# Attention: half of the indexer's head weighting moved from VectorE to GpSimd

## The reference, cut to what matters

```
iq = (x @ w_iq.T + b_iq).reshape(B, S, 4, 64); ik = x @ w_ik.T + b_ik; iw = x @ w_iw.T + b_iw
head_scores  = relu(einsum('bqhd,bkd->bhqk', iq, ik))       # four heads, 256 x 256 each
index_scores = einsum('bhqk,bqh->bqk', head_scores, iw)     # weigh each head per row, add the four
top_idx = top_k(index_scores, 32)                           # the 32 largest of each row stay
logits = (Q @ K.T) * scale, -inf outside top_idx            # Q, K with rotary embedding
x = x + (softmax(logits) @ V) @ w_o.T + b_o
```

## Time and profile before

| | |
|---|---|
| median of 3 runs | 1355.04 us |
| the profiled execution | 1355.75 us |
| its span (first to last instruction) | 1353.9 us |
| PE / ACT / DVE / POOL busy over the span | 78% / 55% / 69% / 60% |
| attention in the trace | from about 16.6 to 210.4 us |
| DVE busy from 100 to 140 us, inside attention | 38.68 of 40 us |
| POOL busy in the same 40 us | 14.62 us |
| TensorE's granted clock from 30 to 180 us | 1.00 |

### The profile page before, as it was taken

How to read it: one execution, slowest core, us unless ns; L and a number is a source line. 1 busy time by engine, 2 the same in 40 slices (tenths; PEclk the granted TensorE clock), 3 DMA queues, 4 the chain that set the end, 5 groups by cost and what they waited for, 6 DMA issues and landing times. The chain is left out here.

```text
span 1353.9 us, 20321 instructions
## 1 busy us (share of the span) xinstructions
PE 1060.0 (78%) x4202; PEld 618.8 (46%) x4203; DVE 932.1 (69%) x2276; ACT 745.8 (55%) x1821; POOL 817.2 (60%) x602
## 2 busy tenths in 40 slices
PE   3898874349999955888989888897775319999995
PEld 3666653227777731333333333333223215555563
DVE  4999997503333333799999999989997625555573
ACT  3777754325555547858586776757531115555542
POOL 1443320667317557877886888788781567437276
PEclk9999985569999976989999999899897559999997
DMA  8994000136425425344435443443540026535335
GB/s 243 161 147 139 1 1 1 41 53 88 71 56 89 84 31 110 85 141 133 155 116 168 124 157 124 137 159 114 185 140 1 31 54 94 85 73 96 79 67 103
DMA packets 136875, 133.22 MB, mean 98 GB/s; under 512 B 14578, under 2 KB 117602, under 8 KB 136674
## 3 DMA queue, kind: packets, MB, share of 16 engines
q1 hardware_dynamic: 107106, 115.55, 32.3%
q0 software_dynamic: 29696, 16.86, 9.8%
HBM read 98.66 MB, written 31.60 MB: 96 GB/s over the span
## 5 line engine op out<-in xcount | busy, mean ns | idle before, releaser
L1569 POOL TENSOR_TENSOR ss_HC<-ss_Hs,ss_Cb 128x512 f32<-128x512 f32 x256 | 317.8, 1273 | 92.1 <-PE ss_Y L1343 70.9
L1343 PE MATMUL ss_Y<-ss_HC,g_ident 128*128 128x512 f32 x512 | 268.7, 643 | 45.5 <-POOL ss_HC L1569 38.0
L1638 DVE TENSOR_TENSOR_SCAN ss_Hs<-ss_dA,ss_dBu 128x512 f32<-128x512 f32 x256 | 297.3, 1204 | 7.0 <-ACT ss_dA L1485 7.0
L992 PE MATMUL m_x_UP<-g_m_w,m_x_gT 128*128 (+1 forms) x532 | 203.9, 489 | 5.9 <-issue 2.9
L1485 ACT ACTIVATE ss_dA<-ss_delta,g_A 128x510 f32<-128x510 f32 x256 | 168.0, 714 | 55.3 <-DVE ss_Hs L1638 54.9
L1343 PEld LDWEIGHTS ss_Y<-ss_HC,g_ident 128*128 128x128 f32 x512 | 90.4, 197 | 206.7 <-POOL ss_HC L1569 147.9
L1630 DVE TENSOR_TENSOR ss_dBu<-ss_duP,ss_Bb 128x512 f32<-128x512 f32 x256 | 163.4, 685 | 21.0 <-DMA ss_Bb<-bc_rows 16.8
L1012 PEld LDWEIGHTS m_x_DP<-g_m_w,m_x_hT 128*128 128x128 f32 (+1 forms) x908 | 131.0, 189 | 80.4 <-issue 41.2
L1012 PE MATMUL m_x_DP<-g_m_w,m_x_hT 128*128 (+3 forms) x908 | 161.5, 296 | 5.9 <-ACT m_x_hT L1068 3.4
L1095 DVE SCALAR_TENSOR_TENSOR m_x_hid<-m_x_UP,m_x_G,m_x_sg 128x352 f32<-128x352 f32 x78 | 45.5, 584 | 151.2 <-ACT m_x_sg L1050 147.6
L972 POOL DMA_INDIRECT g_X<-out_rows,g_slot x64 | 99.2, 1550 | 78.4 <-DMA out_rows<-m_x_YO 55.8
(11 more groups left out here) (242 smaller groups left out, 1869.8 us busy)
## 6 DMA issues: line engine op xcount, KB each, us to landing
ss_Bb<-bc_rows SPq DMA_DIRECT2D x64, 512.0 KB, 4.9
ss_Cb<-bc_rows SPq DMA_DIRECT2D x64, 512.0 KB, 4.1
rows<-g_Z SPq DMA_DIRECT2D x2, 5031.0 KB, 54.2
m_x_G<-rows SPq DMA_DIRECT2D x156, 64.5 KB
out_rows<-m_x_YO SPq DMA_DIRECT2D x156, 64.0 KB
g_m_w<-in_w_up SPq DMA_DIRECT2D x1, 2816.0 KB, 10.7
g_m_b<-in_b SPq DMA_DIRECT2D x1, 2160.0 KB, 11.2
g_X<-in_x SPq DMA_DIRECT2D x4, 512.0 KB, 5.8
```

Source lines behind the costliest of these rows:

```text
L992: ins = nc.tensor.matmul(UP[v % 2][:, at:at + n], gT[v % 2][:], w.w[:, ds(e + c, n)], start=True, stop=True)
L1343: ins = nc.tensor.matmul(Yp[:, h, :], ident[:], HC[n % 2][:, h, :], start=False, stop=n == N - 1)
L1569: nc.gpsimd.tensor_tensor(HC[n % 2][:, h, :], Hs[n % 4][:, h, :], Cb[g % 2][:, n % 2, :], ALU.mult).then_inc(hc_ready.sem, 1)
L1638: v_.tensor_tensor_scan(Hs[n % 4][:, h, :], dA[n % NA][:, h, :, :].rearrange("p s t -> p (s t)"), dBu[:, h, :], 0.0, ALU.mult, ALU.add).th ...
```

## The change

Two new buffers of SBUF, `WG` (doubled) and `W3`, and two semaphores. GpSimd, at the end of its step s and behind the sum of `QK`, waits for the head weights and for R of sequence s, multiplies heads 2 and 3 of each tile with their weights (four TENSOR_SCALAR of 128x256) and adds the two products of both tiles in one 128x512 addition. VectorE weighs heads 0 and 1 alone (two L370 and two L373 per step) and adds GpSimd's share with two TENSOR_TENSOR additions of 128x256 (`join_shares`). Its order within a step becomes: index_scores(s-1), update(s-3), join_shares(s-1), choose rounds 0 to 2, head_weights(s), choose round 3, mask(s-1). ACT's relu waits for both readers of R.

```
+        WG = [m.sb(f"WG{v}", [P, 2 * S]) for v in range(2)]
+        W3 = m.sb("W3", [P, 2 * S])
...
-        idx = m.sig("idx", 8)
+        idx = m.sig("idx", 6)
+        shares, shared = m.sig("shares", 4), m.sig("shared")
...ACT, before the relu of tile t
-                                act.wait_ge(idx.sem, idx.after(s - 1, 7 + t))
+                                act.wait_ge(idx.sem, idx.after(s - 1, 3 + t))
+                                act.wait_ge(shares.sem, shares.after(s - 1, 2 * t + 2))
...VectorE
-                    for h in range(IH):
+                    for h in range(IH // 2):
...
+                def join_shares(s, v):
+                    for t in range(2):
+                        dst = WK[v][:, t * S:(t + 1) * S]
+                        dve.wait_ge(shared.sem, shared.after(s))
+                        dve.wait_ge(idx.sem, idx.after(s, t + 3))
+                        nc.vector.tensor_tensor(dst, dst, WG[v][:, t * S:(t + 1) * S], ALU.add).then_inc(idx.sem, 1)
...
                     if middle:
                         index_scores(s - 1, u)
-                        choose(s - 1, u, range(0, 1))
                     if tail and not (isinstance(s, int) and s < 3):
                         update(s - 3, u)
                     if middle:
-                        choose(s - 1, u, range(1, TOPK // 8))
+                        join_shares(s - 1, u)
+                        choose(s - 1, u, range(TOPK // 8 - 1))
                     if front:
                         head_weights(s, v)
                     if middle:
+                        choose(s - 1, u, range(TOPK // 8 - 1, TOPK // 8))
                         mask(s - 1, u)
...GpSimd, at the end of its step
+                        pool.wait_ge(iw_copied.sem, iw_copied.after(s))
+                        for t in range(2):
+                            pool.wait_ge(relu_ready.sem, relu_ready.after(s, t + 1))
+                            if s >= 2 and t == 0:
+                                pool.wait_ge(idx.sem, idx.after(s - 2))
+                            for k in range(2):
+                                src = R[t][:, k * 512 + S:k * 512 + 2 * S]
+                                nc.gpsimd.tensor_scalar((WG[v], W3)[k][:, t * S:(t + 1) * S], src, IW[v][:, t, IH // 2 + k:IH // 2 + k + 1], None,
+                                                        ALU.mult).then_inc(shares.sem, 1)
+                        pool.wait_ge(shares.sem, shares.after(s))
+                        nc.gpsimd.tensor_tensor(WG[v][:], WG[v][:], W3[:], ALU.add).then_inc(shared.sem, 1)
```

More of the change, by code:

```diff
@@ L363, in index_scores @@
                     dve.wait_ge(iw_copied.sem, iw_copied.after(s))
-                    for h in range(IH):
+                    for h in range(IH // 2):
                         for t in range(2):
                             dst = WK[v][:, t * S:(t + 1) * S]
-                            src = R[t][:, h % 2 * 512 + h // 2 * S:h % 2 * 512 + (h // 2 + 1) * S]
+                            src = R[t][:, h * 512:h * 512 + S]
                             if h == 0:
@@ L371, in index_scores @@
                             else:
-                                dve.wait_ge(idx.sem, idx.after(s, 2 * h - 1 + t))
+                                dve.wait_ge(idx.sem, idx.after(s, t + 1))
                                 ins = nc.vector.scalar_tensor_tensor(dst, src, IW[v][:, t, h:h + 1], dst, ALU.mult, ALU.add)
                             ins.then_inc(idx.sem, 1)
+                def join_shares(s, v):
[4 more added lines that the diff above has]
+                        nc.vector.tensor_tensor(dst, dst, WG[v][:, t * S:(t + 1) * S], ALU.add).then_inc(idx.sem, 1)
                 def choose(s, v, rounds):
@@ L381, in choose @@
                             if k == 0:
-                                dve.wait_ge(idx.sem, idx.after(s, 7 + t))
+                                dve.wait_ge(idx.sem, idx.after(s, 5 + t))
                                 dve.sem_inc(passed, 1)
```

## The result

The changed kernel takes 1395.19 us (median of 4, 1392.60 to 1400.26) against 1355.27 us for the kernel before (4 runs): the ratio of its times is 1.030, with a 95% interval of 1.028 to 1.032. The forecast was 1390 us, range 1349 to 1415.

The account below looks back on a forecast made before the run. VectorE's list of work in attention was taken as the bound; 14 steps x 2.4 us gave +34, the first step +3, the tail -1 to -2, sum +35, from 1355.0 to 1390 us, range 1349 to 1415.

Parts of the forecast that it names:

- VectorE's list: Attention: VectorE's own work sets the pace, 11.04 us a step before, 10.14 us after the change.
- the first rival: Attention: no holding that matters, 10.70 us a step, about 1350 us; chance 0.2.
- The holding: Attention: VectorE instructions with operands in SBUF stand still until GpSimd's current instruction on SBUF is over.
- One sign that the prediction had set against itself: Attention weighing: L373 keeping 481 ns beside GpSimd's shares would mean holding is wrong and time near 1350.
- The sum, 13.4 us a step: VectorE's attention step: 10.14 + 1.0 + 2.3, about 13.4 us against 11.02.
- the product: GpSimd's 2.36 us product in attention holds a join on VectorE, adding 2.0 to 2.4 us a step.
- the third rival: Attention: GpSimd's share costs 0.9 us or more, 14 to 15 us a step, about 1405 to 1415; chance 0.1.
- Joins escape: Attention: joins held but escape the product, 10.9 to 11.6 us a step, around 1359; chance 0.2.
- point of decision: Attention joins: whether the second join has begun at `negmax` + 2.8 us, when GpSimd's product starts.
- the prediction's remark on the clock: TensorE in attention: PE idles some 3 us a step; were it granted less clock, some products would come later.
- The drain: End of attention, where no product comes any more: gives back 1 to 2 us.
- the ring of PE and ACT: Attention: ACT and PE waiting for each other, 10.70 us a step, so a faster VectorE gives at most 0.33.

Follow-up runs that it names:

- e4: Changed kernel without GpSimd's four products and their sum; VectorE weighs two heads and joins a buffer of zeros: 1347.56 us, ratio 0.995.
- e1: Changed kernel with one more wait: GpSimd's rotary product of s starts only after VectorE's joins of s-1: 1364.14 us, ratio 1.007.
- e3: Changed kernel whose joins read their second input from PSUM (the logits) instead of GpSimd's share, waiting for both: 1366.28 us, ratio 1.008.
- e5: Changed kernel with GpSimd's four TENSOR_SCALAR replaced by two TENSOR_TENSOR of 128x512, head weights broadcast: 1391.25 us, ratio 1.025.
- e6: e5 together with the wait of e1 (rotary product behind the joins): 1368.08 us, ratio 1.010.
- e8: e7 with VectorE's head weights one round of the choice earlier, before the last two: 1367.37 us, ratio 1.009.
- e7: e1 with GpSimd's bias addition also waiting for the joins, so nothing of GpSimd's runs beside them: 1359.55 us, ratio 1.004.
- e2: Changed kernel's order alone: VectorE weighs all four heads, no GpSimd share, no joins: 1356.41 us, ratio 1.001.

## Why the prediction was right

**The bound, VectorE's list.** It held: with VectorE's list shortened as in the change and nothing to hold it, e4 gives 10.69 us a step and 1347.6 us, near the first rival's 10.70 and 1350.

**The holding.** Shown by e1 and e3, from both sides: move the product away, or take one input of the join out of SBUF, and the join has its own length. The range of what is held is narrower than forecast. A two-input instruction of GpSimd holds TENSOR_SCALAR, SCALAR_TENSOR_TENSOR and TENSOR_TENSOR of VectorE (e5, e6, e8); GpSimd's TENSOR_SCALAR holds none of them for its length: in the changed kernel and e8 the most that they last longer beside it is 0.27 us (the mask in e8, 699 ns against 427). The Trainium skill, "SBUF — State Buffer", section "Who interferes with whom", says that a VectorE instruction with two SBUF inputs contends with a GpSimd instruction that reads SBUF, one in a two-port mode with GpSimd, and that the one that issues second is fully blocked for the other's whole instruction. For GpSimd's TENSOR_TENSOR the trace agrees (the second join, 2.58 us). For its TENSOR_SCALAR it differs: L377, with two inputs, overlaps one 17 times in the changed kernel and lasts 471 to 474 ns in 16 of them, 687 in one; the measurement decides.

One sign that the prediction had set against itself came true all the same: L377 kept its 479 ns beside the shares, which was to mean that there is no holding and a time near 1350. The sign was ill chosen, for it looked at GpSimd's TENSOR_SCALARs, and the holding came from its TENSOR_TENSORs. The rows from which the holding was read, show only TENSOR_TENSORs of GpSimd (multiplications, which the prediction calls additions).

**The sum, 13.4 us a step.** 13.44 was measured as a mean (13.5 to 13.7 in twelve of the steps with the long join, 14.0 in one, 11.38 in the one without). The largest term, the product, was right; what stands before the joins was wrong in kind and came out near in size by luck. In the step shown, 13.54 us:

| | forecast | measured |
|---|---|---|
| VectorE's own list | 10.14 | 10.18, the rest of 13.54 (e7's 10.88 less 0.15 and 0.53 gives 10.20) |
| held by shares, their sum and the bias addition | 1.0 | 0.67: 0.15 for L374 beside the shares, 0.52 for the first join under the bias addition |
| waiting for the share | 0 | 0.53 |
| the product | 2.3 | 2.16 for the second join |

The joins run from 153.90 to the next MAX8 at 157.25, 3.35 us where e4 has 0.67; 0.52 and 2.16 are the parts of the difference. The prediction let the sum of the shares hold VectorE for 0.4 to 0.6 us, and that did not come: the sum began at 152.34, when the last weighing was already under way, and it was GpSimd's sum that took 1.53 us in place of 1.27. In its place stood the wait for `shared`, 0.53 us, because a share takes 0.93 or 1.08 us and not 0.50: a TENSOR_SCALAR on GpSimd is dearer than the two-input addition of 0.73, above both ends of the forecast. That is the third rival's condition (0.9 us or more). Its 14 to 15 us did not follow, because the `QK` sum never got between the joins.

"Joins escape" fell by its own point of decision, in all steps but the one at 47.26. There its 10.9 to 11.6 us did come, 11.38, but not for its reason: not VectorE was early, TensorE's clock was low and the product late, as the prediction's remark on the clock allowed.

**The ends.** The first step cost 3.8 us (forecast 3). The drain gave nothing back: +1.3 instead of -1 to -2. After the last `IW` now stands one round more (1.44), which the new order moved there, and less of the weighing (0.9); I had counted the second and not the first. e2, which has the order alone, takes 20.05 us from its last `IW` to the end of attention, against 18.55 before. The wait for the share (0.53) and L374 (0.15) make up nearly all of the rest.

**What stayed open.** Whether GpSimd's TENSOR_SCALAR spares VectorE because it has one input or for another reason, and why it now and then costs 0.2 us all the same; no run took it apart. The order in which the two engines get in (bias addition, first join, product, second join, `QK` sum) looks like turns taken, which would be why the sum never came between the joins; it is read from the timeline and not tested.

## What to carry to other kernels

Before work is moved to GpSimd, list which of VectorE's instructions have two inputs in SBUF or are TENSOR_SCALARs, and where in the step GpSimd's two-input instructions lie. Where GpSimd comes first, the meeting costs VectorE the rest of GpSimd's instruction, and a 2.4 us one (2.16 us lost) costs more than the whole help (0.9 us here). A wait that keeps the long one behind VectorE's instruction gave back 31 of the 40 us (e1), and an input in PSUM freed the join (e3), but no version here that uses GpSimd's shares is faster than the kernel before. Busy time doesn't show it, since the held instruction counts as busy (37.73 of 40 us); compare means with those of the same instruction where GpSimd is idle. And look for the next bound first: here the ring of PE and ACT allowed 0.33 us a step at best.

## What the runs showed of the hardware that I had not expected

- GpSimd's TENSOR_SCALAR of 128x256 with a weight per partition takes 0.92 us where nothing meets it and 1.04 to 1.15 beside VectorE's; a two-input addition of the same size takes 0.73. A TENSOR_TENSOR of 128x512 whose second input is one value broadcast over 256 takes 1.04, less than the 1.27 of one with two full inputs and little more than half of what two TENSOR_SCALAR take.
- GpSimd pays as well: its sum L480 has 1.51 us in place of 1.27, the product 2.52 in place of 2.36. In the step shown the sum began while a weighing of VectorE was under way, and the product while the first join was.
- TensorE's granted clock fell from 1.00 to 0.50 after it had stood idle for 4 us at 41 us, and its projections took 3.78 us in place of 1.99; that kept the product away from the joins of that step.
